# Reading the attention scores of one head out of PSUM in pairs of banks

## What is computed

```python
x = x + 0.5 * ffn(layernorm(x))
# attention, per batch (4) and head (16): T = 1024 queries and keys, head size 8
q, k = apply_rotary(q), apply_rotary(k)
scores = einsum('bhqd,bhkd->bhqk', q, k) * 8 ** -0.5
weights = softmax(scores, axis=-1)
attn = einsum('bhqk,bhkd->bhqd', weights, v)
x = x + attn_merged @ out_w + out_b
x = x + 0.5 * ffn(layernorm(x))
```

## Time and profile before

| | us |
|---|---|
| median of 3 runs | 1325.09 (1322.58 to 1326.47) |
| the profiled execution | 1324.05 |
| its span from first to last instruction | 1322.1 |
| TensorE busy | 1269.0 (96%) |
| VectorE busy | 1112.9 (84%) |
| ScalarE busy | 809.9 (61%) |
| attention stage, as the profile shows it | about 385 to 1018 |

### The profile page before, as it was taken

One profiled execution on the slowest core, in us unless ns is written; L12 is line 12 of the kernel. 1 busy time (PEld: TensorE's weight loads), 2 busy tenths in 40 slices (PEclk: granted clock), 3 DMA queues, 4 the chain that ended last, 5 costly groups with the idle time before them and its releaser, 6 DMA issues.

```text
span 1322.1 us, 32042 instructions
## 1 busy us (share of the span) xinstructions
PE 1269.0 (96%) x10240; PEld 616.0 (47%) x10240; DVE 1112.9 (84%) x2306; ACT 809.9 (61%) x1540; POOL 143.4 (11%) x450
## 2 busy tenths in 40 slices
PE   6999999999889999999999999999999999999998
PEld 3666666667522222222222222222223776767776
DVE  7888867887789999999999999999994787777775
ACT  4433333333239999999999999999997333333332
POOL 1020122111221111111111111111110000000000
PEclk9999999999969999999999999999998999999999
DMA  7010111011211100101101011010010100000000
GB/s 207 1 30 19 49 49 48 12 37 49 67 54 32 42 31 31 40 30 39 32 30 40 31 31 40 30 40 31 31 54 14 35 27 27 27 27 21 13 9 9
DMA packets 52265, 48.49 MB, mean 37 GB/s; under 512 B 10080, under 2 KB 44768, under 8 KB 52192
## 3 DMA queue, kind: packets, MB, share of 16 engines
q1 hardware_dynamic: 52192, 47.61, 12.4%
HBM read 23.86 MB, written 23.33 MB: 36 GB/s over the span
## 4 chain that ended last, share of the span: by engine, by line
PE 89%; DVE 5%; issue 4%; ACT 1%; DVEq 0%; DMA 0%; ACTq 0%; SPq 0%
PE ps L765 23%; PE ps L906 22%; PE ps L893 21%; PE ps L752 16%; PE ps L722 2%; PE ps L864 1%; PE ps L742 1%; DVE X L1092 1%; PE ps L686 1%; PE ps L883 1%; PE ps L729 1%; ACT probs L661 1%; DVE mx L1235 1%; DVE act L1080 1%; PE ps L759 1%
## 5 line engine op out<-in xcount | busy, mean ns | idle before, releaser
L1235 DVE TENSOR_REDUCE mx<-ps 128x1 f32<-128x1024 f32 x512 | 591.7, 1217 | 35.9 <-PE ps L864 30.0
L661 ACT ACTIVATE probs<-ps 128x512 f32<-128x512 f32 x1024 | 562.4, 597 | 60.7 <-PE ps L893 42.6
L590 ACT ACTIVATE sg<-ps,unscale 128x512 f32<-128x512 f32 x256 | 173.8, 687 | 307.2 <-PE ps L765 283.0
L906 PE MATMUL ps<-probs,vh 128*32 128x256 f32 x4096 | 330.7, 395 | 16.9 <-issue 11.5
L893 PE MATMUL ps<-Q,K 51*128 51x512 bf16 x1024 | 333.3, 386 | 0.9 <-ACT probs L661 0.5
L864 PE MATMUL ps<-K,Q 48*128 48x512 bf16 x1008 | 327.1, 389 | 2.9 <-DVE mx L1235 2.5
L752 PEld LDWEIGHTS ps<-w,act 128*128 128x128 f32 x2048 | 247.9, 192 | 17.1
L752 PE MATMUL ps<-w,act 128*128 128x128 f32 x2048 | 249.0, 275 | 0.0
L1080 DVE SCALAR_TENSOR_TENSOR act<-ps,unscale,sg 128x512 f32<-128x512 f32 x256 | 183.3, 744 | 60.0 <-ACT sg L590 19.2
L765 PE MATMUL ps<-x_hi,w_hi 128*128 128x512 f16 x512 | 195.6, 382 | 9.9 <-DVE act L1080 6.4
L1092 DVE SCALAR_TENSOR_TENSOR X<-ps,rw,X 128x128 f32<-128x128 f32 (+1 forms) x512 | 143.9, 343 | 62.4 <-PE ps L752 61.8
(11 more groups left out here) (84 smaller groups left out, 608.9 us busy)
## 6 DMA issues: line engine op xcount, KB each, us to landing
o_parts<-ot SPq DMA_DIRECT2D x64, 128.0 KB, 1.9
q_stack<-parts SPq DMA_DIRECT2D x48, 128.0 KB, 2.3
k_stack<-parts SPq DMA_DIRECT2D x48, 128.0 KB, 2.3
Q<-q_stack SPq DMA_DIRECT2D x64, 96.0 KB, 2.3
K<-k_stack SPq DMA_DIRECT2D x64, 96.0 KB, 2.3
probs<-w_in SPq DMA_DIRECT2D x8, 256.0 KB, 4.3
att<-o_parts SPq DMA_DIRECT2D x16, 128.0 KB, 2.6
rden<-rdens SPq DMA_DIRECT2D x16, 128.0 KB, 2.5
```

Source lines behind the costliest of these rows:

```text
L590: nc.scalar.activation(sg[:, j, :], hid[2 * j], ACT.Silu, scale=unscale[:, e, 2 + j:3 + j]).then_inc(silu_done, 1)
L661: nc.scalar.activation(probs[:, kb % PSLOTS, j * CH:(j + 1) * CH], score[i], ACT.Exp, scale=SCALE).then_inc(probs_ready, 1)
L906: last = nc.tensor.matmul(opsum[VW * c:VW * (c + 1), :], vh[:, u % 2, kb, :], probs[:, kb % PSLOTS, c * QW:(c + 1) * QW], start=(kb == 0), ...
L1235: nc.vector.tensor_reduce(mx[:, u % 2, t:t + 1], pair.rearrange("p a b -> p (a b)"), AX_X, ALU.max).then_inc(max_read, 1)
```

## The change

ScalarE now reads the banks 0 and 1 together wherever two neighbouring pieces stand in them, with one exponential of 128 x 1024, and bank 2 alone, with one of 128 x 512. PAIR_STARTS comes out as 0, 3, 6, 8, 11 and 14: the pieces (0,1), (3,4), (6,7), (8,9), (11,12) and (14,15) are pairs, and 2, 5, 10 and 13 are single. A pair waits for both of its pieces, and counts `probs_ready` up by two when it is done. So that the pairs fit, the transposed row moves from place 7 to place 8, which is bank 2. TensorE's code is the same but for MT_AT.

```diff
-MT_AT = 7
+MT_AT = 8
 SCORE_PLACE = [i + (i >= MT_AT) for i in range(HALVES)]
 MT_BANK = MT_AT % SCORE_BANKS
+PAIR_STARTS = [i for i in range(HALVES) if SCORE_PLACE[i] % SCORE_BANKS == 0]
...
+        score_pair = ps[:, 0:2, :].rearrange("p a b -> p (a b)")
+        prob_halves = probs[:].rearrange("p k (j t) -> p (k j) t", j=2)
...
                     if i == MT_AT and more:
                         mrow_copy(r + (u + 1) // QSLOTS, (u + 1) % QSLOTS)
-                    sc.wait_ge(scores_in_psum, HALVES * n + i + 1)
-                    if j == 0:
-                        at_least(sc, probs_used, KB * (n - 1) + kb + 1)
-                    nc.scalar.activation(probs[:, kb % PSLOTS, j * CH:(j + 1) * CH], score[i],
-                                         ACT.Exp, scale=SCALE).then_inc(probs_ready, 1)
+                    if i - 1 in PAIR_STARTS:
+                        continue
+                    wide = i in PAIR_STARTS
+                    end = i + 1 if wide else i
+                    sc.wait_ge(scores_in_psum, HALVES * n + end + 1)
+                    at_least(sc, probs_used, KB * (n - 1) + end // 2 + 1)
+                    to = prob_halves[:, i:end + 1, :].rearrange("p h t -> p (h t)")
+                    nc.scalar.activation(to, score_pair if wide else score[i], ACT.Exp,
+                                         scale=SCALE).then_inc(probs_ready, 2 if wide else 1)
                     if i == 3 and not first:
                         o_copy(r + (u - 1) // QSLOTS, (u - 1) % QSLOTS)
```

More of the change, by code:

```diff
@@ L653, in head @@
                 for i in range(HALVES):
-                    kb, j = i // 2, i % 2
                     if i == MT_AT and more:
                         mrow_copy(r + (u + 1) // QSLOTS, (u + 1) % QSLOTS)
-                    sc.wait_ge(scores_in_psum, HALVES * n + i + 1)
-                    if j == 0:
-                        at_least(sc, probs_used, KB * (n - 1) + kb + 1)
-                    nc.scalar.activation(probs[:, kb % PSLOTS, j * CH:(j + 1) * CH], score[i],
-                                         ACT.Exp, scale=SCALE).then_inc(probs_ready, 1)
+                    if i - 1 in PAIR_STARTS:
[7 more added lines that the diff above has]
+                                         scale=SCALE).then_inc(probs_ready, 2 if wide else 1)
                     if i == 3 and not first:
```

## The result

| | before | after |
|---|---|---|
| median, us (4 runs each) | 1324.63 | 1576.78 (1571.86 to 1584.59) |
| ratio, 95% interval | | 1.1909 [1.1858, 1.1961] |
| the profiled execution, us | 1324.05 | 1571.86 |
| its span, us | 1322.1 | 1569.9 |

The first page of the changed kernel, to set beside the earlier trace rows: busy time of each engine, the chain that ended last, and the groups of lines that changed (L1241 is the reduction of the maxima, L667 the exponentials, L899 the pieces, L912 the products with the values).

What follows compares the result with a forecast made beforehand. TensorE and VectorE were taken as nearly even, kept going by three rotating banks. The serial path of paired banks (205 us alone), with a third of the stage at low clock, adds 279: 1324 + 279 = 1603, forecast 1604, range 1493 to 1705.

Steps and rivals of the forecast that it cites:

- the serial path: Attention stage, pair to pair: exponential, release, refill and restart in six steps; head 13.03 us instead of 9.83, 205 us more.
- the clock: TensorE in the attention stage: a third of the time at half clock, heads averaging 14.2 us, stage 279 us longer.
- The waits: ScalarE, ahead of nearly every exponential of 1024: idle time ended by L899, some 3 to 4 us per head.
- Cost of the wide exponential: ScalarE, exponential of 1024: engine held 0.93 us in place of 0.98, banks released at 1.03 us.
- The products ahead of the second piece: Steps (0,1) to (3,4) and (8,9) to (11,12): products with the values stand inside the refill, 2.46 us each.
- The copy behind (3,4): Step (3,4) to (6,7): the head's first products wait for the ot copy, now behind the pair; 2.71 us.
- two stretches of other work: Kernel before, 364.2 to 372.2 and 1006.0 to 1014.0 us: clock fell to half after TensorE was busy 5.80 and 7.41 of 8.00.
- the first rival: Attention stage: serial path as forecast while TensorE's clock stays up; 1324 + 205 = 1529 us, chance 0.29.
- the 17.3: Attention stage, us per head throughout at low TensorE clock, with TensorE the bound; 478 us over the whole stage.
- The overlap of the refill: Rival, TensorE's products done before the odd piece opening a pair: head 11.14 us, 1408, or 1468 at half; chance 0.08.
- the gain from fewer instructions: Rival, ScalarE's freed 0.3 us per head closes most of VectorE's gap: 1305 us, at most 1293; chance 0.03.
- The one read that would be served as two of 512: Rival, ScalarE's read across two banks: 1.09 us instead of 1.03, 23 us more; chance 0.02.

Runs made afterwards that it cites:

- experiment 2: Changed kernel with each exponential of 1024 made as two of 512, still waiting for both pieces and releasing both banks together; 1575.48 us, ratio 1.1888.
- experiment 1: Kernel before with only the transposed row of maxima moved from place 7 to 8, all exponentials single; 1326.41 us, ratio 1.0016.
- experiment 3: Changed kernel with two exponentials of 512 per pair, the first waiting for both pieces, each releasing its bank at its own end; 1456.85 us, ratio 1.1005.
- experiment 4: Changed kernel with TensorE's products with the values behind pieces 3 and 11 moved one piece later; 1481.29 us, ratio 1.1192.
- experiment 5: Changed kernel with the ot copy ahead of the pair (3,4) instead of behind it; 1497.57 us, ratio 1.1309.
- experiment 9: Changed kernel with TensorE's matmul of the maxima behind piece 5 made five times instead of once; 1560.76 us, ratio 1.1787.
- experiment 8: Changed kernel with the ot copy ahead of the pair (3,4) and the products behind piece 11 one piece later; 1462.78 us, ratio 1.1059.
- experiment 11: Kernel before with TensorE's first products of a head, which wait for the ot copy, behind piece 6 instead of ahead; 1313.69 us, ratio 0.9930.
- experiment 10: Kernel before with the ot copy one exponential earlier, ahead of piece 3; 1334.92 us, ratio 1.0083.

## Why the prediction held

The time, 1576.78, lies in the range, 27 below the forecast of 1604. The mechanism stands as well. That the number is so near is in part luck: two terms had the wrong size, and they went opposite ways, 27 us too little for the serial path and some 54 too much for the clock.

- **What bounds the kernel.** That ScalarE's instruction count buys nothing is shown by experiment 2: with 384 exponentials more, the narrow version of the joint waits costs the same as the wide one. That it is waiting for and releasing one bank at a time that keeps the two nearly even engines going is shown by experiments 1, 3 and 2: 1326 us with both, 1457 without the single wait, 1575 with neither.
- **The waits.** The idle time ahead of the pairs is 4.93 us a head, more than the 3 to 4 expected.
- **Cost of the wide exponential.** Predicted 1.03 us, measured 1.02; predicted distance to the next instruction 0.93, measured 0.92 (700.90, 701.82).
- **The serial path.** Predicted steps 1.80, 2.46 and 2.71; measured 1.85 (1.96 at the change of heads), 2.53 and 2.74. Predicted head 13.03, measured 13.45, so 232 us instead of 205. The mis-sized term is the 0.50 from the last piece's start to the exponential, taken from one of 512: ahead of one of 1024 it is 0.55 to 0.58, some six times 0.06 a head. At the change of heads the two pieces start 0.30 apart instead of 0.22.
- **The products ahead of the second piece** (0.31 + 0.57 us from piece to piece instead of 0.22): experiment 4 took them out and both steps fell to that of their neighbours.
- **The copy behind (3,4):** experiment 5 took it out, and the step fell from 2.74 to 1.85.
- **The clock.** Right in kind: it falls in thin heads at full clock and rises again by itself (experiment 9 for the cause). Wrong in size: I took a third of the stage at the low level and 74 us for it; it was 77 us of low clock more in the whole program, under a tenth of the stage, and some 20 us. The step that failed is the guess of the share. I had read two stretches of other work as no emptier than the new loop and gave their effect to every head. The sign that I set for it, a granted clock below 0.9 over the stage, did not appear: it is 0.97 from 400 to 1220 us, nearer to the 1.00 of the first rival. The work at the low clock was sized well: from piece 10 to piece 12 TensorE takes 1.98 us (833.16, 835.14), as predicted for a key block, and the two steps wholly at 0.50 are longer by 5.89 / 4.38 = 1.34, where 17.3 / 13.0 is 1.33. No whole head of the changed loop at the low clock was compared with the 17.3.
- **The rivals.** The clock that stays up (1529) is nearer to what the path alone makes (1324 + 232 = 1556) than the forecast was, but too low by the 0.42 us per head and the low clock. The overlap of the refill and the gain from fewer instructions have no trace. The one read that would be served as two of 512 would have lasted 1.09 us and lasted 1.02.

Both advices of the Trainium skill that the prediction weighed can be held against this kernel. The larger tile that the Trainium skill advises (Advanced Engine Details and Errata, The Read-Write Bubble) saved 29 us of ScalarE's busy time and none of the program's. The rotation over different banks that the Trainium skill advises (Perfetto Trace Analysis, Optimizing Tensor Performance, Matmuls) is what the pairs gave up, at 252 us with the queues' orders as they stand and 139 with those of experiment 8.

## What to carry to other kernels

A read that spans several banks waits for the last of them and releases all of them at once, so count the sets of banks, not the banks: with one pair and a single bank beside it there is no second buffer for the pair, and each pair puts the whole refill (here 0.8 us at the least, 1.5 and 1.7 with foreign work in the producer's queue) on the path. Look in the producer's queue for what stands between the matmuls of one group; it stood in the same place in experiment 1 and cost nothing there, where the consumer waits for one piece at a time. And where a wait can't be taken away, move the instruction behind the waiting one ahead of it (experiment 11) rather than hurry the engine that is waited for (experiment 10).

## What the runs showed of the hardware

An exponential of 1024 starts 0.56 us after the start of the matmul it waits for (707.46, 708.02), one of 512 in the same place 0.50 (765.22, 765.72, experiment 2). A bank is written again 0.06 us after the exponential that read it has ended (706.51, 706.57). TensorE's granted clock fell to half (1.2 GHz) now and then in a loop whose longest pause was 1.5 us and in which TensorE reads as busy in 609 of 820 us; in the stretch shown it fell inside that pause, ahead of the products at 827.82. With the longest pause of each head filled, busy in 652 of 820, it did so hardly at all, and the program with more work in it was the faster one. A microsecond at the low level cost this loop 0.26 to 0.29 us.
